# One order for each engine's segments of a three-stage pipeline, laid out anew

## The reference, cut to what matters

```
h = frames(x) @ DCT.T
h = h + mamba_both_directions(layernorm(h))  # projection, conv of 4 taps, silu, scan, gate, norm
h = h + experts(layernorm(h))                # 8 experts, 128 -> 512 -> 128, gelu, top 2 by a gate
h = h + window_attention(layernorm(h))       # 8 shifts, softmax over the shifts
h = h + patterns(layernorm(h))               # gelu, top 64 of 512; gelu, top 128 of 256; gelu, top 64 of 512
```

## Time and profile before

| what | us |
|---|---|
| median of 3 runs | 9580.68 (9533.44 to 9596.44) |
| profiled execution, its span | 9575.9 |
| PE busy | 8297.2 (87%) |
| DVE busy | 7809.5 (82%) |
| ACT busy | 3577.3 (37%) |
| POOL busy | 2715.8 (28%) |

### The profile page before, as it was taken

How to read it: one execution, slowest core, us unless ns; L and a number is a source line. 1 busy time by engine, 2 the same in 40 slices (tenths; PEclk the granted TensorE clock), 3 DMA queues, 4 the chain that set the end, 5 groups by cost and what they waited for, 6 DMA issues and landing times.

```text
span 9575.9 us, 125362 instructions
## 1 busy us (share of the span) xinstructions
PE 8297.2 (87%) x40296; PEld 5979.8 (62%) x40296; DVE 7809.5 (82%) x23500; ACT 3577.3 (37%) x6200; POOL 2715.8 (28%) x2124
## 2 busy tenths in 40 slices
PE   6898888998888989888989888988889898889873
PEld 4566666666666666666666666666666666666652
DVE  1298888898888888888888888888888888888888
ACT  1344333344333344333444333443333443333431
POOL 1322233322233222233222233222332222332220
PEclk7778777778777778777788777787777787777875
DMA  1000000000000000000000000000000000000000
GB/s 41 2 1 4 4 4 4 4 1 4 4 4 4 1 4 4 4 4 4 1 4 4 4 4 4 1 4 4 4 4 2 2 4 4 4 4 1 2 2 3
DMA packets 42666, 38.00 MB, mean 4 GB/s; under 512 B 1328, under 2 KB 41360, under 8 KB 41360
## 3 DMA queue, kind: packets, MB, share of 16 engines
q1 hardware_dynamic: 42000, 29.21, 1.0%
HBM read 18.95 MB, written 10.26 MB: 3 GB/s over the span
## 4 chain that ended last, share of the span: by engine, by line
issue 34%; DVE 33%; POOL 19%; PE 11%; ACT 1%; POOLq 0%; DMA 0%; DVEq 0%; SPq 0%; ACTq 0%
DVE work L1008 11%; DVE m L1006 11%; POOL hid L352 4%; PE pM L548 3%; DVE h L950 3%; POOL hid L375 3%; PE pM L559 3%; POOL un L296 3%; POOL hid L367 2%; DVE a L1008 2%; POOL yg L327 2%; PE pD L622 1%; DVE stats L834 1%; POOL u L296 1%; POOL rstd L291 1%
## 5 line engine op out<-in xcount | busy, mean ns | idle before, releaser
L1008 DVE MATCH_REPLACE8 work<-m,work 128x256 f32<-128x256 f32 (+1 forms) x4192 | 2155.2, 522 | 0.0
L1006 DVE MAX8 m<-work 128x8 f32<-128x256 f32 (+1 forms) x4192 | 2013.5, 526 | 8.8 <-issue 8.8
L750 ACT ACTIVATE hid<-pM,cst 128x320 f32<-128x320 f32 x2048 | 1064.0, 527 | 953.5 <-PE pM L548 665.1
L548 PE MATMUL pM<-uT,cst 128*128 128x320 f32 x4096 | 1365.6, 457 | 53.7 <-ACT hid L750 8.3
L291 POOL TENSOR_TENSOR rstd<-vare,mhalf 128x5 f32<-128x5 f32 x160 | 189.6, 1185 | 3832.7 <-DVE vare L839 3832.7
L559 PEld LDWEIGHTS pM<-cst,hid 128*128 128x128 f32 x10240 | 1183.9, 191 | 88.5 <-DVE h L950 55.6
L559 PE MATMUL pM<-cst,hid 128*128 128x128 f32 x10240 | 1201.3, 275 | 21.4 <-DVE h L950 20.7
L548 PEld LDWEIGHTS pM<-uT,cst 128*128 128x128 f32 x4096 | 679.4, 194 | 596.0 <-ACT hid L750 490.9
L438 PE MATMUL pS<-u_fm,wconv_s 128*128 128x315 f32 (+1 forms) x3072 | 895.7, 436 | 8.8 <-ACT xs L712 8.8
L875 DVE TENSOR_TENSOR_SCAN Lt<-pS,cst 121x424 f32<-121x424 f32 x384 | 398.6, 1038 | 606.9 <-PE pS L450 606.5
L474 PE MATMUL pS<-xs,skip 128*128 128x105 f32 x1536 | 557.8, 466 | 375.2 <-DVE Mt L885 273.1
(11 more groups left out here) (195 smaller groups left out, 14416.0 us busy)
## 6 DMA issues: line engine op xcount, KB each, us to landing
x_sb<-in_x SPq DMA_DIRECT2D x32, 256.0 KB
out<-hk SPq DMA_DIRECT2D x32, 256.0 KB
cst<-in_weights SPq DMA_DIRECT2D x2, 2048.0 KB, 11.9
hid<-in_setup SPq DMA_DIRECT2D x1, 1904.0 KB, 20.7
out<-hk SPq DMA_DIRECT2D x32, 57.0 KB
x_sb<-in_x SPq DMA_DIRECT2D x32, 56.5 KB
cst<-in_weights SPq DMA_DIRECT2D x1, 1344.0 KB, 16.9
cst<-in_weights SPq DMA_DIRECT2D x1, 1164.5 KB, 6.1
```

The lines of the kernel that those rows point to most:

```text
L548: nc.tensor.matmul(pM[:, 512 * (n % 2):512 * (n % 2) + W // 2], w1[:, e, j * P:(j + 1) * P], uT[:, lo:lo + W // 2], start=True, stop=True) ...
L750: nc.scalar.activation(hid[:, e % 2, j, lo:lo + W // 2], pM[:, 512 * (n % 2):512 * (n % 2) + W // 2], ACT.Gelu, bias=c("b1")[:, n // 2:n / ...
L1006: link(nc.vector.max(m[i], now[i]), len(tiles) - 1)
L1008: link(nc.vector.match_replace(work[i], m[i], now[i], GONE), len(tiles) - 1 if r or firsts is None else 0)
```

## The change

The four strings are replaced. Each new string holds as many 1s, 2s and 3s as the old one (PE 107, 88, 41; ACT 61, 140, 42; DVE 56, 21, 80; POOL 20, 11, 2). Nothing else is changed: the same instructions with the same waits, in the same order within every stage, stand in another order between stages.

Read against the segments, in the new strings: PE issues its projection units between downs 1 and 5 (before: behind down 8), scan steps 0 to 5 among downs 5 to 9 and steps 6 to 11 behind them (before: all 12 behind the attention's projections). DVE does the gate (L916 to L936) ahead of the first top-k round, the second top-k between the scans, and L960 to L966 behind scan step 8 (before: ahead of step 0). ACT alternates Silu and Gelu accordingly. POOL copies the states of steps 0 to 5 ahead of the norm of the attention (before: that norm first), and runs its sums of the attention behind step 9.

```diff
@@ -80,15 +80,15 @@
 
 
 
-PE_ORDER = ("1333322332212222222222222122222223112232232222232222223222332222232222222322222223222222222112222223"
-            "2332313113111312321222222311111111111311311113111111111111111311111311111311111111111111111111111131"
-            "111111311112111113111113311311133332")
-ACT_ORDER = ("1333322321222222222222222222222222222232222213222222232222222223222222222222222233112332212222222232"
-             "2222222222222222222322222222222222222333332222222222222223333313113111331111123222222111111131311113"
-             "1131111111111111112331131111311113131111332")
-DVE_ORDER = ("2333223231333232333333123331211333233333233323333323333333233321233333333333323331111311111311112111"
-             "311111311131111333311112111121111332111131111332333311333")
-POOL_ORDER = ("231122112112211212122111111211113")
+PE_ORDER = ("13331322223222232222222221221222212112111211221121113212311111321211112211121321231212122111132121112311"
+            "12322222122111132223222221121121221212112212212221221112111112313311131332111121133222212111213131131313"
+            "3111311111111113313333233332")
+ACT_ORDER = ("31323232222322122222222222222222222312222222112121221222111122221211221311121211211112122231112222232112"
+             "22221112131131121322211111223222222222223222223222222223221223232332222221222222222212222222322221133333"
+             "13323122222123133333331211113133332")
+DVE_ORDER = ("32223231332313111333333321333321233332133311331131312133331113133213331213331311311323113312121111331111"
+             "33333111211311333111113313113323333333312321333322333")
+POOL_ORDER = ("231111111121111212211122322211112")
 
 
 def merged(order, *stages):
```

## The result

| | us | per full pass |
|---|---|---|
| before, median of 4 runs on this chip | 9567.57 (9533.44 to 9596.44) | 289.5 |
| after, median of 4 runs | 9721.42 (9720.98 to 9723.36) | 293.6 |
| ratio after to before | 1.0168, interval 1.013 to 1.0205 | |
| profiled execution's span: before, after | 9575.9, 9719.2 | +143.3 in all |

The kernel became 1.7% slower. The forecast was 9835 us, or 2.7% slower; the measured time lies about midway between it and the no-change rival's 9590. One run of this document, of e_new4's four, took 9672.81 us at a mean granted clock of 0.758 for the others' 0.809, and its ratio leaves that run out. First the page of after, which answers to the earlier trace rows.

The account below looks back on a forecast made before the run. DVE and PE were both taken as full in the middle of a pass, with DVE idle 46.5 us mostly at border and scans. 9575.9 + 285 (full passes) - 30 (edge pass) = 9831, so 9835 us; range 9500 to 10130.

Parts of the forecast that it names:

- no-change rival: Whole kernel: clock stays at 2.4 GHz through all scans, waits 4 us, pass 291, time 9590 us; chance 0.22.
- The forecast's 299 us: Length forecast for one full pass: 286.7 us plus 12 us of DVE waits in the scans.
- Border, 80 us: From DVE's last Mt (L885) to the first expert matmul: DVE work, then a serial chain; 58.5 us before.
- my list: DVE's instructions in a row at the pass border, counted as near 48 us without waits.
- work that moves costs what it cost, with two exceptions: Everywhere: reordered instructions keep their durations, except through PE's clock and ACT's activation tables.
- PE's front, 78 us, with waits of 17 for down 3 and about 3.6 for a2: First expert matmul to tile 2's L622: PE work 75 us plus 3 us waiting for ACT; DVE waits there.
- Tables, 33 loads a pass, hidden but for 3 us: ACT, nearly all in PE's front: loads rise from 21 to 33 a full pass, +15.4 us of ACT.
- Scans, 131 us to the next D: From 158.6 us to DVE's next last Mt: 119 us DVE work after the first scan, 12 of waits at half clock.
- much slower rival: Scans among experts pull PE's clock down too: pass 314 us, time 10270 us; chance 0.17.
- Sum, +9.5 a pass: Full pass 299 us against 289.5; over 30 passes +285 us.
- The pass with stages 1 and 2, -30; the others unchanged: Edge passes: the one with stages 1 and 2 takes 232 against 266.9 us, taken as -30; others stay.
- Signs named: Profile after: L950 wait 10 us or more a pass, L875's halved, 33 table loads, border waits near 15 us before L916.

Follow-up runs that it names:

- e_new4: All four strings laid out anew, scan steps 0 to 5 among the experts, no L971 or select beside POOL's two-tile work: 9424.49 us, ratio 0.9878 to before.
- e_new1: All four strings laid out anew, scans behind experts and projections as before, no L971 or select beside POOL's two-tile work: 9348.63 us, ratio 0.98 to before.

## Why the prediction was right, and where it wasn't

The direction held, and the waits that the prediction named are there. But they aren't what made the kernel slower. The forecast's 299 us need DVE idle for 55 us of a pass (299 less 243.6); measured are 45.3, for 45.8 before, so the long waits at the gate and at down 3 only replace the short ones of the scans. What grew is DVE's work, 248.3 us a pass for 243.7, by collisions with POOL, a term that the prediction put at nothing. That "slower" came true, and the time within the range, is in this part luck. Step by step, with what one full pass showed:

- *Border, 80 us:* 84.3. The serial chain and the gate's wait came as described (10.5 us at L916, 4.0 and 3.0 more ahead of it). The missing 4 us are the collisions: L971 5.49 for the 3.0 in my list, the three selects 5.1 for 3.8, and the last two 3.4 for 1.4, in sum 5.8, less what else my list had too long. (The list as written adds up to 43.5 us and not "near 48": it names six rounds of two tiles where eight stand there, and 48 has all eight.) The 3.8 was itself taken from before's trace, where one select of the three is stretched beside POOL's L367:

```profile
4443.54 2.46 DVE L1017 SCALAR_TENSOR_TENSOR a<-work,a 128x512 f32<-128x512 f32 x1
4446.06 0.69 DVE L1017 SCALAR_TENSOR_TENSOR a<-work,a 128x512 f32<-128x512 f32 x1
4446.67 0.69 DVE L1017 SCALAR_TENSOR_TENSOR a<-a 128x512 f32<-128x512 f32 x1
```
The sign stood there and I averaged over it; "work that moves costs what it cost, with two exceptions" needed a third.
- *PE's front, 78 us, with waits of 17 for down 3 and about 3.6 for a2:* 77.9 (4316.17 to 4394.04), 17.24 and 2.1. Right.
- *Tables, 33 loads a pass, hidden but for 3 us:* there are 32, for 21 before. That they cost little is shown for PE's queue as it is (Gelu for Silu: ratio 1.0159 for 1.0168); the cover is PE's work, and with one tap for four the same loads decide (1.0047 to 0.9867).
- *Scans, 131 us to the next D:* 121.7. DVE's waits there were 3.7 us, not 12. This is the step that was mis-sized: I took half clock from step 6 on, since scan instructions alone had 0.52; it was granted in full up to 4485.6, so through steps 6 and 7. The no-change rival had this part right (4 us), but not the border. (The much slower rival's 10270 is mis-added: its own terms, +735 and -30, give 10281.)
- *Sum, +9.5 a pass:* +4.1. From 299: border +4.4, front -0.7 (I had 78.6 with the wait for a2), the first scan +0.5, the rest -9.6 (131.3 to 121.7, of which the waits are 8.3): 293.6. So the rise was forecast at more than twice its size, and the two large errors, waits in the scans that didn't come and collisions that did, have opposite signs.
- *The pass with stages 1 and 2, -30; the others unchanged:* +8.4, wrong, and the pass with stages 2 and 3 grew by 11.0, for a cause that stays open. I had walked the pass with stages 1 and 2 to the end of the scans as if the attention ended with them. The longest of PE's waits behind them, in the list for that stretch:

```profile
PEld pM L595 <- POOL un L296: 20.4, 1, 20.4
```
The attention's sums now stand on POOL behind step 9, and the end of stage 2 is a serial chain behind them that nothing covers here; that stage 3's work covers it in a full pass is my reading. Before's strings in the edge passes brought 266.8 for 275.3 back.
- *Signs named:* L950's wait over 10 us in a pass (17.24), L875's down by more than half (606.5 to 254.6), a wait before L916 (10.5 where I had 15 in all at the border, 17.4 with the other two), and 32 table loads where I had 33: all came. They are signs of the traded waits, and none of them could have told that trade from a loss.

The collisions as the cause of the full passes' +4.1 rest on two runs: one multiplication on POOL gave 3.5 back, order alone 3.3. The 0.6 to 0.8 that is left has no experiment of its own. A kernel with after's order and no stretched select at all was not run; by the three groups (438.1 us against 317.5 in e_new1) the kernel with one multiplication still has 121 us of stretching in it at a ratio of 1.0033, so that after's order without any might stand some 1% below before, if all of it lay on the path. That is worked out, not shown.

## What to carry to other kernels

The order here moved idle time from many short waits to two long ones and won nothing. Before filling a long wait, look for what the chain that ends it waits for: filling two of them made the pass 4.3 and 6.5 us longer, while shortening PE's and ACT's queue ahead together gave 9.2 where each alone gave 3.5 and 0.2. When moving work of DVE, list what POOL does in the same microseconds: instructions of both that read two SBUF tiles hardly overlapped here. A mean over a group hides this, its forms and single durations show it.

## What the runs showed of the hardware that was not expected

- DVE's select of 128x512, with two tiles of SBUF in, took 0.69 us alone and 1.3 to 1.9 in after (2.46 in before) beside POOL's multiplications or sums of two tiles; L971 took 0.81 alone (e_new1) and 1.44 in the mean of after, where half of them stand beside POOL's; POOL's L367 1.43 in the mean of before and 1.85 in that of after. That two inputs on DVE's side are what matters fits the Trainium skill (SBUF — State Buffer, SBUF: two separate sides); in the kernel with the round moved, MAX8 and MATCH_REPLACE8 kept 0.67 to 0.69 us while POOL's four still ran (4202.47 to 4204.98). On POOL's side one tile in wasn't enough: beside L296 the select took 0.71 to 0.73 us.
- The granted clock stayed at 1.00 (2.4 GHz) through scan steps among experts with PE busy 93% (76.45 of 82.00 us), where scan steps alone had 0.52 with PE busy 87%. In the run with the filled wait it stayed there for 133.1 us for after's 146.8.
